# Cross-attention and a recurrent feed-forward on one Trainium2 core: 18 of the second norm's transposes through memory and VectorE instead of TensorE

## What is computed

```python
def _xattn_ref(q, k, v, W_proj, b_proj):          # heads of 32, |i - j| <= 64
    scores = jnp.einsum('bhqd,bhkd->bhqk', qh, kh) * scale
    attn = jax.nn.softmax(jnp.where(dist > WINDOW, -jnp.inf, scores), axis=-1)
    return jnp.einsum('bhqk,bhkd->bhqd', attn, vh) ... @ W_proj.T + b_proj

def step(c, xt):                                  # one step for each of the 8 batches
    ft = sigmoid(xt @ wf.T + c @ uf.T + bf)
    it = sigmoid(xt @ wi.T + c @ ui.T + bi)
    gt = tanh(xt @ wc.T + c @ uc.T + bc)
    return ft * c + it * gt

x = x + _xattn_ref(_layernorm(x), ctx, ctx, W_proj, b_proj)
x2 = _layernorm(x)
c_final = scan(step, c0, x2)
out = x + tanh(x2 @ wo.T + c_final @ uo.T + bo)
```

## Time and profile before

| | |
|---|---|
| median of 3 runs | 956.67 us (954.79 to 958.66) |
| the profiled execution, its own time | 956.46 us |
| its span | 954.6 us |
| granted TensorE clock, mean | 0.997 of full |
| TensorE busy | 924.4 us, 97% |
| VectorE busy | 664.2 us, 70% |
| ScalarE busy | 476.3 us, 50% |
| GpSimd busy | 202.9 us, 21% |
| DMA | 114.15 MB in 99604 packets, 66728 of them under 2 KB, 9384 under 512 B |

### The profile page before, as it was taken

One profiled execution on the slowest core, in us unless ns is written; L12 is line 12 of the kernel. 1 busy time (PEld: TensorE's weight loads), 2 busy tenths in 40 slices (PEclk: granted clock), 3 DMA queues, 4 the chain that ended last, 5 costly groups with the idle time before them and its releaser, 6 DMA issues.

```text
span 954.6 us, 21946 instructions
## 1 busy us (share of the span) xinstructions
PE 924.4 (97%) x7888; PEld 723.1 (76%) x7888; DVE 664.2 (70%) x2263; ACT 476.3 (50%) x1430; POOL 202.9 (21%) x228
## 2 busy tenths in 40 slices
PE   5889999899999999999999999999999999999998
PEld 3545666688888888888888888888888888878887
DVE  6888898878779877897789867986798522142222
ACT  5887667655445544655545546555555412131222
POOL 4475322211111111111111111111111000003444
PEclk9999999999999999999999999999999999999999
DMA  9554422233333334333433234333322040049862
GB/s 287 166 163 149 117 88 75 67 104 93 95 107 116 108 104 111 106 107 106 115 109 100 83 104 117 95 85 84 96 85 68 24 154 1 1 161 389 294 246 100
DMA packets 99604, 114.15 MB, mean 120 GB/s; under 512 B 9384, under 2 KB 66728, under 8 KB 97960
## 3 DMA queue, kind: packets, MB, share of 16 engines
q1 hardware_dynamic: 98776, 112.47, 37.8%
q10 hardware_dynamic: 720, 0.27, 0.2%
HBM read 82.98 MB, written 29.74 MB: 118 GB/s over the span
## 4 chain that ended last, share of the span: by engine, by line
PE 88%; DVE 4%; ACT 3%; issue 3%; POOL 1%; DMA 1%; SPq 0%; DVEq 0%; ACTq 0%; POOLq 0%
PE ps_g L633 18%; PE ps_g L635 17%; PE ps_g L634 17%; PE ps_a L670 5%; PE ps_a L692 5%; PE ps_m L633 4%; PE ps_v L713 3%; PE ps_m L635 3%; PE ps_m L634 3%; PE ps_m L745 2%; PE ps_v L718 2%; ACT probs L841 2%; PE ps_a L633 2%; PE ps_a L635 2%; PE ps_a L634 2%
## 5 line engine op out<-in xcount | busy, mean ns | idle before, releaser
L841 ACT ACTIVATE probs<-probs,rowmin 128x192 f32<-128x192 f32 (+1 forms) x512 | 239.5, 470 | 87.7 <-DVE rowmin L948 87.6
L948 DVE CUSTOM_DVE_ANT_0 probs<-ps_a,mask 128x192 f32<-128x192 f32 (+1 forms) x512 | 167.3, 386 | 50.5 <-PE ps_a L670 49.7
L883 ACT ACTIVATE gate<-ps_g,bias 128x512 f32<-128x512 f32 x84 | 57.7, 687 | 183.5 <-PE ps_g L635 183.1
L633 PE MATMUL ps_g<-state_hi,gate_w 128*128 128x512 f32 x336 | 133.5, 397 | 0.0
L635 PE MATMUL ps_g<-state_hi,gate_w 128*128 128x512 f32 x336 | 131.1, 390 | 0.0
L634 PE MATMUL ps_g<-state_lo,gate_w 128*128 128x512 f32 x336 | 130.8, 389 | 0.0
L983 DVE STREAM_TRANSPOSE keys<-probs 32x128 f32<-32x128 f32 x420 | 126.0, 300 | 5.4 <-issue 0.2
L841 ACT ACTIVATION_READ_ACCUMULATOR probs<-probs,rowmin 128x1 f32 x512 | 96.4, 188 | 0.0
L612 POOL TENSOR_TENSOR attn_lo<-recip,attn_hi 128x512 fp32r<-128x512 f32 x23 | 29.8, 1294 | 283.4 <-ACT attn_hi L854 283.4
L846 ACT ACTIVATE probs_t<-ps_a 128x512 f32<-128x512 f32 x108 | 59.4, 595 | 51.9 <-PE ps_a L692 51.9
L633 PE MATMUL ps_g<-x2t_even,gate_w 128*128 128x512 f32 x192 | 80.0, 417 | 0.0
(11 more groups left out here) (203 smaller groups left out, 1723.2 us busy)
## 6 DMA issues: line engine op xcount, KB each, us to landing
values<-ctx_rows SPq DMA_DIRECT2D x34, 256.0 KB, 4.4
xr<-x SPq DMA_DIRECT2D x32, 256.0 KB, 3.9
keys<-ctx_t SPq DMA_DIRECT2D x16, 512.0 KB, 4.9
x_dram<-xr SPq DMA_DIRECT2D x32, 256.0 KB, 5.4
gate_w<-x2t_dram SPq DMA_DIRECT2D x8, 1024.0 KB, 10.0
keys<-ctx_t SPq DMA_DIRECT2D x16, 384.0 KB, 3.5
x2t_dram<-x2t_even SPq DMA_DIRECT2D x12, 512.0 KB, 3.9
x2t_dram<-x2t_odd SPq DMA_DIRECT2D x12, 512.0 KB, 3.9
```

What stands on the lines that cost most here:

```text
L633: pe.matmul(ps, lhs[0], rhs[0], start=start, stop=False)
L841: act.activation(row, row, ACT.Exp, bias=rowmin[:, i % 2, h:h + 1], scale=-1.0, accum_out=rowsum[:, i // G % 2, i % G, h:h + 1]).then_inc( ...
L883: act.activation(gate[:, min(gt, 1), :], ps_g[i % 2][:, :], ACT.Tanh, bias=(first_bias if b == 0 else bias)[:, gt, m:m + 1], scale=1.0 if ...
L948: dve.tensor_tensor_reduce(probs[:, i % 2, h, 0:SEEN[t]], ps_a[h][:, score_at[i]:score_at[i] + SEEN[t]], mask[:, MASK0[t]:MASK0[t] + SEEN[ ...
```

## The change

`x2` of 18 tiles is no longer transposed by TensorE. `MOVED` holds tiles 8 to 30 except each batch's last (11, 15, 19, 23, 27): tiles 8, 9, 10, 12, 13, 14 and so on to 28, 29, 30. Such a tile is written to DRAM and read back so that 32x32 blocks change place; VectorE then turns each block. The `turn2` and `turn2_lo` steps of these tiles move from the first third of the second double slot to its end. The queries of tile 10, the last that TensorE turns in a double slot, move behind the residual of the tile before. No arithmetic changes.

```diff
+    MOVED = [j for j in range(SENT - 1, TILES) if j % TT < TT - 1]
...
             cells(2)
-            if s == 0 and i + 1 < TURNED_X:
-                tile_steps("query", i + 1)
-            if s == 2:
+            if s == 2 and i - 1 not in MOVED:
                 tile_steps("turn2", i - 1)
...
             if s == 0 and i + 1 >= TURNED_X:
                 tile_steps("query_norm", i + 1)
+            if s == 0 and i + 1 < TURNED_X:
+                tile_steps("query", i + 1)
+                tile_steps("query_out", i + 1)
             gates()
             cells(7)
             if s == 0:
                 tile_steps("ln2b", i - 1)
             else:
+                if i - 1 in MOVED:
+                    tile_steps("turn2", i - 1)
+                    tile_steps("turn2_lo", i - 1)
                 if i + 2 < TILES:
                     steps.append(("norm_rows", i))
...
# SyncE, ln2b, after the store of the residual rows
+                    if i in MOVED:
+                        sp.wait_ge(x2_done, i + 1)
+                        if t == 0:
+                            sp.wait_ge(gate_sum, UNITS * (b - 1))
+                            sp.wait_ge(x2t_out[b % 2], DMA * TT * (b // 2))
+                        sp.dma_start(x2_dram[i], x2[:, :]).then_inc(x2_sent, DMA)
+                        sp.wait_ge(x2_sent, DMA * moved(i + 1))
+                        for a in range(P // BLK):
+                            blocks = x2_dram[i, BLK * a:BLK * (a + 1), :].rearrange("r (k m c) -> m r k c", m=P // BLK, c=BLK)
+                            home = x2t[b % 2][:, 1, :, t * P + BLK * a:t * P + BLK * (a + 1)]
+                            sp.dma_start(home.bitcast(F32), blocks).then_inc(x2_moved, DMA)
...
# SyncE, norm_rows
-                    sp.wait_ge(x2_turned, i)
+                    sp.wait_ge(x2_turned, by_tensor(i))
+                    if i - 1 in MOVED:
+                        sp.wait_ge(x2_lo, i)
...
# TensorE
-                if kind == "turn2":
+                if kind == "turn2" and i not in MOVED:
...
# ScalarE, turn2
+                    if i in MOVED:
+                        act.wait_ge(x2_blocks, moved(i + 1))
+                        act.activation(x2t[b % 2][:, 0, :, t * P:(t + 1) * P], x2[:, :].rearrange("p (k q) -> p k q", k=G),
+                                       ACT.Copy).then_inc(x2_hi, 1)
+                        continue
...
# VectorE
+                if kind == "turn2" and i in MOVED:
+                    b, t = i // TT, i % TT
+                    dve.wait_ge(x2_moved, moves_landed(i + 1))
+                    dve.transpose(x2[:, :].rearrange("p (k q) -> p k q", k=G),
+                                  x2t[b % 2][:, 1, :, t * P:(t + 1) * P].bitcast(F32)).then_inc(x2_blocks, 1)
...
                     dve.wait_ge(x2_hi, i + 1)
+                    if i in MOVED:
+                        dve.tensor_tensor(x2t[b % 2][:, 1, :, cols], x2[:, :].rearrange("p (k q) -> p k q", k=G),
+                                          x2t[b % 2][:, 0, :, cols].bitcast(F32), ALU.subtract).then_inc(x2_lo, 1)
+                        continue
```

More of the change, by code:

```diff
@@ L21, in bass_xattn_ffn @@
 def bass_xattn_ffn(nc, x, x_t, ctx_rows, ctx_t, w_proj, b_proj, w_gates, u_gates, biases, w_out, u_out, b_out, in_c,
-                   out, x1_dram, x2t_dram, recip_dram):
+                   out, x1_dram, x2_dram, x2t_dram, recip_dram):
     B, T, D = x.shape
@@ L73, in bass_xattn_ffn, with moved, moves_landed, by_tensor @@
     PAIR = 2
+    MOVED = [j for j in range(SENT - 1, TILES) if j % TT < TT - 1]
+    def moved(n):
+        return sum(j < n for j in MOVED)
+    def moves_landed(n):
+        return DMA * (P // BLK) * moved(n)
+    def by_tensor(n):
+        return n - moved(n)
     chunks = [(gt, u, k) for gt in range(NG) for u in (1, 0) for k in range(0, G, PAIR)]
@@ L167, in bass_xattn_ffn @@
                 tile_steps("load_v", i + 1)
-                tile_steps("query_out" if i + 1 < TURNED_X else "load_q", i + 1)
+                if i + 1 >= TURNED_X:
+                    tile_steps("load_q", i + 1)
             else:
@@ L391, in bass_xattn_ffn @@
         recip_sent = sem("recip_sent"); recip_in = sem("recip_in")
-        xt_in = sem("xt_in"); norm_in = sem("norm_in")
+        xt_in = sem("xt_in"); norm_in = sem("norm_in"); x2_sent = sem("x2_sent"); x2_moved = sem("x2_moved")
         raw_in = sem("raw_in"); bo_in = sem("bo_in")
@@ L405, in bass_xattn_ffn @@
         attn_t = sem("attn_t"); x1_done = sem("x1_done")
-        stat2 = sem("stat2"); aggr2 = sem("aggr2"); var2 = sem("var2"); x2_done = sem("x2_done"); x2_lo = sem("x2_lo")
+        stat2 = sem("stat2"); aggr2 = sem("aggr2"); var2 = sem("var2"); x2_done = sem("x2_done"); x2_lo = sem("x2_lo"); x2_blocks = sem("x2_blocks")
         in_gate = sem("in_gate"); kept = sem("kept"); cell = sem("cell"); c_lo = sem("c_lo")
@@ L642, in _ @@
                     if i > SENT:
-                        pe.wait_ge(x2_lo, i - 2)
-                        pe.wait_ge(recip_out, SENT)
+                        pe.wait_ge(x1_done, i - 1)
                     else:
@@ L749, in _ @@
                         if i + 1 >= SENT:
-                            pe.wait_ge(q_ready, min(i + 3, TURNED_X))
+                            pe.wait_ge(q_ready, min(i + 2, TURNED_X))
                             pe.wait_ge(x2_lo, i)
@@ L861, in _ @@
                     b, t = i // TT, i % TT
-                    act.wait_ge(x2_turned, i + 1)
+                    if i in MOVED:
[3 more added lines that the diff above has]
+                        continue
+                    act.wait_ge(x2_turned, by_tensor(i + 1))
                     if t == 0 and b >= 2:
@@ L926, in _ @@
                     if i > SENT:
-                        dve.wait_ge(x2_turned, i - 2)
+                        dve.wait_ge(x2_turned, by_tensor(i - 2))
                     if i - 2 < WHOLE:
@@ L1012, in _ @@
                     dve.wait_ge(q_turned, min(i + 3, TURNED_X))
-                    need(dve, x2_turned, i)
+                    need(dve, x2_turned, by_tensor(i))
                     if i + 2 >= TURNED_X:
@@ L1142 @@
     B, T, D = arrays["x"].shape
+    x2_dram = nc.dram_tensor("x2_dram", (B * T // P, P, D), F32, kind="Internal").ap()
     recip_dram = nc.dram_tensor("recip_dram", (B * T // P, HEAD, P), F32, kind="Internal").ap()
@@ L1146 @@
                    [d["w_c"], d["w_i"], d["w_f"]], [d["u_c"], d["u_i"], d["u_f"]],
-                   [d["b_c"], d["b_i"], d["b_f"]], d["w_out"], d["u_out"], d["b_out"], d["in_c"], out, x1_dram, x2t_dram,
-                   recip_dram)
+                   [d["b_c"], d["b_i"], d["b_f"]], d["w_out"], d["u_out"], d["b_out"], d["in_c"], out, x1_dram, x2_dram,
+                   x2t_dram, recip_dram)
     r = run_bass_kernel_spmd(nc, [arrays], core_ids=[0])
```

## The result

| | before | changed |
|---|---|---|
| median of 6 runs, us | 956.04 (954.79 to 958.66) | 1006.14 (1001.73 to 1008.85) |
| ratio, 95% interval | | 1.0521 (1.0492 to 1.0550) |
| span of the profiled execution, us | 954.6 | 1005.3 |
| mean granted clock | 0.997 | 0.981 |

The change costs 50 us. The forecast was 1015, the range 980 to 1125. It came within 9 us in part by luck: TensorE's waits were put 16 us too high, and the saving and the clock, off by 3.6 and 4.6 us the other way, hid half of that.

The account below looks back on a forecast made before the run. TensorE was taken to bound the kernel, one stream without a gap from tile 8 to 30. Waits net of the saving, +48.2, and the clock, +10.2, on 956.46 gave 1014.9, so 1015 us; range 980 to 1125.

Parts of the forecast that it names:

- Few engines for the blocks: Block DMAs, outermost dimension 4, were to stay on some four of 16 DMA engines: 6.1 us for 256 KB.
- Step 3: Tile 20's four block DMAs: 2048 pieces of 128 B at 43 GB/s take 6.1 us, there at 521.3.
- steps 1 and 2: Tile 20's x2 store lands at 513.5 behind line 510's broadcast and the residual's store; block DMAs issue at 513.6.
- Where VectorE stands: VectorE reaches tile 20's new transpose at 517.7, waits 3.6 us; then 2.2 us to the low half, blends 1.4, six sides.
- first kind: Moved tiles that are first of their batch: TensorE +4.7 us each, six tiles 28.2, plus 10.2 for the clock.
- "hidden" rival: 16 engines and 1.6 us less on VectorE cover every wait, the whole 9.5 us remain: 947; chance 0.04.
- The clock: A 3.6 us TensorE wait behind each first tile of a batch costs 1.7 us at half clock: 10.2; others nothing.
- third kind: Moved tiles that are third of their batch, such as 22: TensorE +1.7 us each, five tiles 8.5, no clock loss.
- The query at 0: Moving tile 10's query, 0.53 us of TensorE in another place: between -1 and +2 us, taken as 0.
- Small reads slower: Rival: 128 B pieces read from DRAM cost what 512 B ones do, blocks take 14 us: 1168; slower pieces 0.18.
- Sixteen engines: Rival: blocks spread over 16 engines, landed at 517.4 before VectorE arrives; first tiles +1.1 us each: 957; chance 0.11.
- The prices in the cover of `norm_rows` and the loads: Unpriced: later norm_rows and loads of keys, values, queries; were the cover gone, VectorE would wait up to 3 us.

Follow-up runs that it names:

- e1: The changed kernel with the block exchange moved to four stores of 32 outermost rows, then one load of 128 rows in 512 B pieces: 955.69 us, ratio 0.9998.
- e7: The exchange of e1, with VectorE's transpose, copy and low half moved to a first double slot where VectorE has room: 947.16 us, ratio 0.9906.
- e3: The changed kernel with only the six first tiles of a batch moved (8, 12, ... 28): 987.95 us, ratio 1.0342.
- e4: The changed kernel with MOVED empty, so only the query of tile 10 moves and TensorE transposes every x2: 953.60 us, ratio 0.9979.
- e8: e7 with the query of tile 10 back where it stood before the change: 949.65 us, ratio 0.9938.

## Why the prediction was right, and where not

The forecast of 1015 had the mechanism and the place right, and was 9 us above the median. Its terms against the profiled executions of before and after, in us (the forecast's waits are taken without what it saved: 6 x 5.23 + 6 x 2.53 + 5 x 2.23, since each stood net of 0.53):

| term | forecast | measured | from |
|---|---|---|---|
| TensorE's waits behind moved tiles | +57.7 | +41.4 | 26.7 + 12.8, and 1.9 behind tile 30 |
| four transposes less on 18 tiles | -9.5 | -5.9 | 18 x 0.33 |
| half clock | +10.2 | +14.8 | half of TensorE's busy time in the eight stretches, 16.5, less 1.7 before |
| waits of tile 10's query | 0 | -1.6 | 2.41 before, 0.51 + 0.27 now |
| sum | +58.4 | +48.7 | spans: +50.7, so 2.0 stay open |

**Few engines for the blocks: right.** The share was 0.32 for 5.3 us, and with the blocks off the few engines the wait went (`e1`, with the limits said there). What was mis-sized is the rate. Step 3 took 43 GB/s at a share of 0.28 from a window of 0.38 us; over the four DMAs it was 52 at 0.32, the work of five engines rather than four. Why five, the runs don't tell. The blocks took 5.3 us, not 6.1. The first packets came 1.1 us after issue, not 1.4. The store of `x2` landed 6.4 us behind the residual's issue, where steps 1 and 2 had 6.2. In sum 13.3 instead of 13.9 us for tile 20.

**Where VectorE stands: right.** It waited 2.98 us for tile 20, forecast 3.6. The pieces behind it held within 0.2 us: 0.71 for the transpose (0.7), 2.1 from its start to the end of the low half (2.2), 1.3 for the blends (1.4), 1.88 for `sides`.

**The waits of TensorE: right in place, too large in size.** From the residual's store to the second `value` product it was 14.72 us before for tile 20 (507.39 to 522.11) and is 18.64: +3.9, forecast +4.7. Tiles 21 and 22 give +1.6 and +1.0, forecast +2.0 and +1.7. They are short by 0.8, 0.4 and 0.7 us, and of that the path from the residual's store to the transpose makes 0.6, 0.3 and 0.7 (13.3, 13.6 and 13.2 us instead of 13.9). Not all six of the first kind are alike either: tile 8 waits 1.23 + 1.40, tile 20 2.61 + 1.33.

**Tile 30: missed.** "Behind tile 30 no slot follows that needs `sides`; there the 0.53 is simply saved." The projection behind it needs the low half, and TensorE stood 1.91 us for it (820.14, releaser line 1064), with 3.4 us at half the clock behind. VectorE's wait was the longest of all there, 7.23 us, since nothing else was left for it to do.

**The saving: 0.33, not 0.53.** The distance between two starts in the stream is the price of an instruction only where its successor would start as soon without it. Here `score` starts 0.07 us later behind a cell product than the transposes did, and more is lost further on. It made the "hidden" rival's 947 unreachable by its own working: it needed 9.5 us. `e7` comes to 947 with 5.9 from the transposes and the rest from the query.

**The clock: right in kind, too small, and for the first kind right by luck.** 1.7 us for each of six tiles came from one row. The first kind lost 11.4 us, forecast 10.2, but not as forecast: nothing behind tile 8, 3.4 us of half clock behind two tiles, 6.8 behind three. The other 3.4 us are the stretches behind tile 14, a third kind, and tile 30, which the prediction left at nothing (the stretch at 125 us stands against the 1.7 of before). What decides between 3.4 and 6.8 us stays open: behind waits of 2.44 + 1.39, 2.61 + 1.33 and 2.56 + 1.30 us it was 6.8, behind 3.68 + 0.28 and 3.15 + 0.28 us 3.4, but in `e3` 6.8 behind 3.22 + 0.28.

**The query at 0: wrong.** Two rows in the prediction's own groups held the answer: the earlier trace rows has the wait of 2.41 us at the very instruction that the change moves, and the earlier trace rows its half-clock stretch. They were read as evidence on the clock only. `e4` gives 1.8 us. In the profiled execution of before the stretch was there, so the 1.7 taken off in the table's clock row fits that execution and not every one.

**The rivals.** Small reads slower: refuted, pieces of 128 B took 0.32 x 16 x 5.3 us / 2048 = 13 ns each on an engine. Sixteen engines: not this kernel, but `e1` comes near to it by another pair of transfers, 955.7 against its 957, with its wait of 1.1 us at its place. That rival had the last of the four issues 1.8 us behind the first; here it was 2.9 behind, and whether more engines would have brought it forward wasn't tested. The prices in the cover of `norm_rows` and the loads: VectorE waited 16.8 us for `queries` in this stretch instead of 5.3, and none of it reached TensorE, as its list of waits shows only the rows above.

## What to carry to other kernels

Before work moves through memory, look at which DMA stands ahead on the queue: one broadcast with an outermost dimension of 4, split into four DMAs, took four fifths of this loss away. Then place the consumer where its engine has slack: the faster trip alone only came back to the time of before, and with the consumer moved too it was 0.94% below (moving it without the faster trip wasn't tried; 0.62% of the 0.94 stay without the query move, `e8`). And read each wait in a profile of before against the diff: if the change moves the instruction that waits, the wait is a term of the sum.

## What the chip showed that was not expected

- Issuing a DMA took longer behind others of its kind. A block DMA with 512 pieces of 128 B from DRAM held SyncE's queue for 1.14 to 1.16 us (median of 36 each), but the first of tile 20's four for 0.53 us and all four for 4.08; the plain store of 256 KB held it for 0.33 us. The four stores of `e1` with as many pieces took 0.63 us each (median of 72), 2.66 us together. Whether the issues stood behind the few engines or something else was not tested.
- Behind line 510's transfer the store of `x2` took 5.3 us to land, and 2.5 us where that transfer was split in four. Each of the two moves 256 KB.
- The length of a stretch at the lower clock followed neither the length of the wait nor its pieces. Waits of 2.61 and 1.33 us stood with 6.8 us at 0.50, waits of 3.68 and 0.28 us with 3.4, and in `e3` waits of 3.22 and 0.28 us with 6.8 again.
